# A gated cross-attention and FFN block on one core: the projection six slots behind instead of seven, and the last slots and the product stage's end in another order

## The chip, the core and the metric

The kernel runs on one of the eight cores of a Trainium2 chip. The core has five instruction queues: TensorE (PE in the profile; PEld is its weight load), VectorE (DVE), ScalarE (ACT), GpSimd (POOL) and SyncE (SP, which only issues transfers here). They run side by side and meet at semaphores. PSUM is the memory that TensorE writes into, SBUF the working memory. The metric is the device time of one execution in microseconds; the kernel before has a median of 463.42 us over 3 runs (462.39 to 464.57).

## What is computed

With x of 4 batches x 1024 rows x 256 columns and a context c of 4 x 154 x 256, cut from the reference:

```python
x = x + tanh(g_x) * xattn(layernorm(x), c, w_sim, b_sim, W_qv, b_qv)
x = x + tanh(g_f) * ffn(layernorm(x), w_gate, w_up, w_down)

# xattn(h, c): d = 256
Sim  = (h @ w1)[:, :, None] + (c @ w2)[:, None, :] + einsum('bid,bjd->bij', h * w3, c) + b_sim
A    = softmax(Sim, axis=2);  hq = A @ c
Batt = softmax(max(Sim, axis=2), axis=1);  hc = sum_i Batt_i h_i          # one row per batch
out  = concat([h, hq, h * hq, h * hc]) @ W_qv + b_qv

# ffn(y): weights quantized to 4 bits in blocks of 32, activations to 16 bits over the whole tensor
y = q16(y); up = q16(y @ q4(w_up).T); gate = q16(y @ q4(w_gate).T)
gate = q16(gate * u16(sigmoid(gate)));  o = q16(gate * up);  return o @ q4(w_down).T
```

Two things tie the stages together. The row `hc` of a batch needs the scores of all of the batch's 1024 rows before any of its rows can be projected. And each `q16` needs the largest magnitude of a whole 4096-row tensor before the next stage can begin.

## The kernel before, in words

**The attention stage** (to about 200 us) works in slots. A slot m has one pair of 128-row tiles at each step of a pipeline; there are N = 16 pairs, four to a batch, so slot m is place s = m mod 4 of batch b = m div 4. In a slot TensorE turns h of pair m (`turn_h`, line 521), scores pair m-1 (`score`, 535), turns the attention weights of pair m-2 (`turn_a`, 544), attends for pair m-3 (`attend`, 554), projects pair m-LAG (`project`, 566 to 570, twelve matrix products) and turns the normalized result of pair m-LAG-1 (`turn_y`, 609). LAG is 7. Each engine has a loop over the slots of its own, in which a fixed order of calls is written out; nothing is scheduled by a tool. Every engine takes its instructions strictly in that order, so a wait holds up all that stands behind it.

What VectorE does in a slot: `attended` (1135, the product h*hq of pair m-4), `residual` (1143 to 1154: x plus the projection, then mean and variance), `scored` (1119, bias and row maximum), `stats` (1081 to 1088), `normed` (1127), `norm_x1` (1160, the normalized yb) and `max_y` (1200). `row_std` and `y_std` (384, 388) are the reciprocal roots, which GpSimd takes; `bias_x` (439) adds the bias to x on GpSimd.

Once per batch: `batch_max` on VectorE (1206, 1208) makes a diagonal of the row maxima, `batch_max` on TensorE (629) spreads it, `batch_shift` (1212) reduces it, `batch_exp` on ScalarE (902) makes the weights, ScalarE and GpSimd multiply four rows of h each (908, 414), `row_pair` and `row_add` on GpSimd (421 to 431) sum them, `batch_cols` on TensorE (636, 637) sums over partitions, and `summary` on VectorE (1216 to 1224) makes the weights `we`, which the third part of each projection (570, or 601 in a batch's first pair) reads. A batch's first pair is projected in two parts, `project_first` (589, 591), which does not need `we`, and `project_rest` (601), which does.

In the gaps the FFN weights are quantized, one matrix m = 0, 1, 2 after the other: `weight_scales` (DVE 1238 to 1243), `weight_max` (PE 643), `weight_unit` (DVE 1248 to 1253), `weight_q` in two halves (POOL 401), `weight_values` (DVE 1258), `weight_f` (ACT 913) and `weight_n` (POOL 407). They stand in the slots that `W_AT` gives. One scale tile `wsc` serves all three. Then nine `turn_w` (PE 663) transpose the weights through three PSUM banks; ScalarE copies the high half out (918) and VectorE's `weight_part` (1264) makes the low half, which frees the bank for the `turn_w` three further on. `TURN_AT` says in which slots they stand.

**The hidden stages** (about 200 to 389 us) are three passes of 12 units of matrix products (731, 736): gate, up, and up once more, for the product. **The product stage** takes |up| of a unit (`up_int`, ACT 1020), its signs (DVE 1453) and the maximum of the product (DVE 1459, 1469). **The down stage** (from 396 us) quantizes chunks of 256 rows (ACT 1050/1054, DVE 1504 to 1509) and multiplies them with w_down (PE 766; the first chunk 777 and 782). Between the last hidden unit and the first chunk TensorE runs `WARM` = 22 products that nobody reads (803).

Of the kernel before, what the change touches and what calls it, by code (L numbers as in the profile page):

```python
# [38 lines left out]
P = 128  # L39
# [27 lines left out]
def build(nc, x, ctx, g_xattn, g_ffn, w_sim, b_sim, w_qv, b_qv, w_gate, w_up, w_down, out):  # L67
# [86 lines left out]
    wsc = place(a, "wsc", [P, NB], F32)  # L154
    wri = place(a, "wri", [P, NB], F32)
# [57 lines left out]
    with ExitStack() as stack:  # L213
# [29 lines left out]

        wchain, wall_rdy, wdiag_rdy, wm_ps, wri_rdy, wq_rdy, wqi_rdy, wqf_rdy, wn_rdy, wt_ps, wth_rdy, wt_rdy = map(
# [9 lines left out]
        gbank_ps, ubank_ps, aubank_rdy = map(sem, ("gbank_ps", "ubank_ps", "aubank_rdy"))  # L254
# [33 lines left out]
        TURNS = [(1, 0), (1, 1), (1, 2), (0, 0), (0, 1), (0, 2), (2, 0), (2, 1), (2, 2)]  # L288
        TURN_AT = {17: (0,), 19: (1, 2), 20: (3, 4, 5), 21: (6, 7, 8)}
# [87 lines left out]
        def _(pool):  # L377
# [17 lines left out]
            def weight_q(m, i):  # L395
# [5 lines left out]
                pool.tensor_tensor(wm, wm, wri[:, n].unsqueeze(2).broadcast_to([P, NB // 2, QB]), ALU.mult).then_inc(wq_rdy, 1)  # L401

            def weight_n(m):

                pool.wait_ge(wqf_rdy, m + 1)
                wm = wr[:, m, :].rearrange("p (n k) -> p n k", k=QB)
                pool.tensor_tensor(wm, wm, wsc[:].unsqueeze(2).broadcast_to([P, NB, QB]), ALU.mult).then_inc(wn_rdy, 1)  # L407
# [36 lines left out]
            for m in range(N + LAG):  # L444
                b, s = m // NP, m % NP
                if s == 3 and 4 <= m < N + 4:
                    for n in range(2):
                        bias_x(m - 5 + n)
                if s == 1 and 1 <= b <= B:
                    row_weigh(b - 1)  # L450
                if LAG <= m < L + LAG:
                    y_std(m - LAG)
                if s == 1 and 1 <= b <= B:
                    row_pair(b - 1)
                if s == 2 and 1 <= b <= B:
                    row_add(b - 1)
                if 1 <= m and m + 3 < N:
                    row_std(m + 3)
                if s == 0 and 4 <= m < N + 4:
                    for n in range(2):  # L460
                        bias_x(m - 4 + n)
                for i in range(3):
                    if m in (W_AT[i], W_AT[i] + 1):
                        weight_q(i, m - W_AT[i])
                    if m == W_AT[i] + 2:
# [30 lines left out]
        def _(pe):  # L496
            def turn_context(b):
                pe.wait_ge(cx_in[b], 16)
                ge(pe, ngm_rdy, b - 1)
                ge(pe, hc_rdy, b - 2)  # L500
# [130 lines left out]
            def batch_cols(b):  # L631

                pe.wait_ge(hs_rdy, b + 1)
                pe.wait_ge(cxT_rdy, min(b + 3, B))
# [10 lines left out]
            def turn_w(i):  # L645
# [3 lines left out]
                if i == 0:  # L649
                    pe.wait_ge(hT_rdy, N)  # L650
                elif i == 1:
# [26 lines left out]
            for m in range(N + LAG):  # L678
                b, s = m // NP, m % NP
                late = s == 3  # L680
                if LAG <= m and not late:
# [899 lines left out]
```

## Time and profile before

| | us |
|---|---|
| median of 3 runs | 463.42 |
| the profiled execution | 465.64 |
| its span, first to last instruction | 463.8 |
| TensorE busy | 436.0 (94%) |
| VectorE busy | 366.3 (79%) |
| ScalarE busy | 274.0 (59%) |
| GpSimd busy | 111.2 (24%) |
| mean granted TensorE clock | 0.982 |

Busy times are sums over instructions. TensorE's products overlap each other, and their ends are modelled, so its cost is best read from the starts of consecutive groups. The granted clock is the share of TensorE's full clock that it was given. The page's 40 slices show TensorE at 9 tenths or more nearly everywhere, with three places below: the first slice, the slices around 139 to 175 us (clock digits 8, 9, 6), and the slice at 390 us.

### The profile page before, as it was taken

Reading aid. Unit: us, or ns where it says so; the run is one execution under the profiler, and the core shown is the slowest. Engines: PE = TensorE matmul, PEld = TensorE weight load, DVE = VectorE, ACT = ScalarE, POOL = GpSimd, SP = SyncE. Lnnn points to the kernel's source line nnn. Section 1 sums busy time; section 2 is a strip of 40 time slices with the busy share of each in tenths; the row PEclk is TensorE's granted clock in tenths of the full one; section 3 lists DMA queues with packets and bytes.
Section 4 is the critical chain, followed back from the end, with each engine's and each line's share of the span. In section 5 each row is a group of like instructions: output and inputs, shape, how many; then the busy total and the mean of one; then the engine's idle time right before and its main releaser. Section 6 shows DMA issues by size and latency. Waiting matters only on the chain.

```text
span 463.8 us, 6761 instructions
## 1 busy us (share of the span) xinstructions
PE 436.0 (94%) x2430; PEld 299.2 (64%) x2430; DVE 366.3 (79%) x650; ACT 274.0 (59%) x342; POOL 111.2 (24%) x109
## 2 busy tenths in 40 slices
PE   4799999999997959999999999999999999899997
PEld 3788889799886848744444444444444444688886
DVE  5886789788785878886433789999898888798874
ACT  2677364457522312284334599998287777977760
POOL 1239275364743553100000013344000000000000
PEclk9999999999998969999999999999999999899999
DMA  7940002000200100110000000000000000344442
GB/s 243 315 155 1 0 2 91 1 0 6 87 1 0 65 28 0 38 54 0 0 0 0 1 1 1 0 0 0 1 0 0 0 0 1 114 137 137 136 136 69
DMA packets 20672, 21.13 MB, mean 46 GB/s; under 512 B 825, under 2 KB 20392, under 8 KB 20648
## 3 DMA queue, kind: packets, MB, share of 16 engines
q1 hardware_dynamic: 20628, 20.82, 14.2%
q8 instruction: 14, 0.23, 0.2%
q14 instruction: 10, 0.08, 0.1%
q10 hardware_dynamic: 20, 0.00, 0.0%
HBM read 12.43 MB, written 8.39 MB: 45 GB/s over the span
## 4 chain that ended last, share of the span: by engine, by line
PE 43%; DVE 26%; issue 20%; ACT 7%; POOL 4%; DMA 1%; ACTq 0%; POOLq 0%; DVEq 0%
PE ps L766 12%; PE ps L731 9%; PE ps L736 5%; DVE cols L1414 4%; DVE yb L1160 4%; PE ps L566 2%; PE ps L570 2%; PE ps L568 2%; PE ps L601 2%; DVE hid L1430 2%; ACT hid L991 2%; PE ps L554 1%; POOL wr L407 1%; POOL h L414 1%; ACT ag L996 1%
## 5 line engine op out<-in xcount | busy, mean ns | idle before, releaser
L731 PE MATMUL ps<-xh,wuh 128*128 128x512 f16 x192 | 72.8, 379 | 1.2 <-DVE gq L1453 1.1
L731 PE MATMUL ps<-xh,wul 128*128 128x512 f16 x192 | 72.8, 379 | 0.0
L736 PE MATMUL ps<-xl,wuh 128*128 128x512 f16 x192 | 57.1, 379 | 0.0
L1393 DVE TENSOR_REDUCE cols<-hid x10 | 22.9, 2286 | 24.3 <-ACT hid L968 24.3
L766 PE MATMUL ps<-wdl,oh 128*128 128x256 f16 x168 | 37.4, 273 | 0.0
L766 PE MATMUL ps<-wdh,oh 128*128 128x256 f16 x168 | 37.4, 273 | 0.0
L731 PE MATMUL ps<-xh,wgh 128*128 128x512 f16 x96 | 36.4, 379 | 0.0
L731 PE MATMUL ps<-xh,wgl 128*128 128x512 f16 x96 | 36.4, 379 | 0.0
L968 ACT ACTIVATE hid<-ps 128x2048 f32 x10 | 18.8, 1875 | 27.5 <-PE ps L736 27.5
L731 PEld LDWEIGHTS ps<-xh,wuh 128*128 (+1 forms) x192 | 18.8, 98 | 24.5 <-issue 2.2
L472 POOL PARTITION_ALL_REDUCE cols<-cols x4 | 1.5, 366 | 136.1 <-DVE cols L1353 130.0
L736 PEld LDWEIGHTS ps<-xl,wuh 128*128 (+1 forms) x192 | 18.8, 98 | 22.7
L731 PEld LDWEIGHTS ps<-xh,wul 128*128 (+1 forms) x192 | 18.8, 98 | 22.4
L1050 ACT ACTIVATE oq<-hid,cols 128x1536 int16 (+1 forms) x15 | 23.6, 1572 | 11.7 <-DVE ol L1509 11.7
L554 PE MATMUL ps<-aT,cx 77*128 77x256 f32 x128 | 30.5, 381 | 0.0
L1453 DVE TENSOR_TENSOR gq<-gq,ps 128x2048 bf16<-128x2048 int16 x11 | 25.2, 2287 | 6.0 <-ACT au L1020 6.0
L838 ACT ACTIVATE hT<-ps 128x512 f32<-128x512 f32 x16 | 9.5, 591 | 34.0 <-PE ps L521 34.0
L1430 DVE CUSTOM_DVE_ANT_0 hid<-ag,sq 128x2048 f32<-128x2048 int16 x12 | 29.2, 2435 | 0.2
L1414 DVE TENSOR_REDUCE cols<-ps 128x1 f32<-128x2048 f32 x12 | 27.4, 2286 | 1.6 <-PE ps L736 1.6
L736 PE MATMUL ps<-xl,wgh 128*128 128x512 f16 x96 | 28.6, 379 | 0.1
L1160 DVE TENSOR_SCALAR yb<-xa,cols 128x256 f32<-128x256 f32 x30 | 23.9, 836 | 5.4 <-POOL cols L388 5.4
L388 POOL TENSOR_TENSOR cols<-cols 128x2 f32<-128x2 f32 x15 | 11.7, 777 | 60.4 <-DVE cols L1154 60.4
(222 smaller groups left out, 1064.1 us busy)
## 6 DMA issues: line engine op xcount, KB each, us to landing
x_scratch<-xa SPq DMA_DIRECT2D x4, 1024.0 KB, 4.4
xo<-x_scratch SPq DMA_DIRECT2D x16, 256.0 KB, 2.7
out_dram<-xo SPq DMA_DIRECT2D x15, 256.0 KB, 2.2
xa<-in_x SPq DMA_DIRECT2D x3, 1024.0 KB, 12.6
xa<-in_x SPq DMA_DIRECT2D x4, 256.0 KB, 4.1
wv<-in_L_xattn_W_qv SPq DMA_DIRECT2D x1, 1024.0 KB, 8.5
wr<-in_L_ffn_w_gate SPq DMA_DIRECT2D x1, 768.0 KB, 10.2
wr<-in_L_ffn_w_up SPq DMA_DIRECT2D x1, 768.0 KB, 11.6
```

The lines of the kernel that those rows point to most:

```text
L388: pool.tensor_tensor(rstd2, vp2, mhalf[:, 0:2], ALU.pow).then_inc(rstd2_rdy, 1)
L554: mm = pe.matmul(hq_bank[:, d * PT:(d + 1) * PT], cx[b][0:JP, k, d * P:(d + 1) * P], aT[0:JP, n % 3, k, :], start=k == 0, stop=k == 1)
L731: pe.matmul(ps[hf][:, q, :], w_[:, d, ds(k * P, P)], xh[:, d, n], start=d == 0 and w_ is wh, stop=False)
L736: mm = pe.matmul(ps[hf][:, q, :], wh[:, d, ds(k * P, P)], xl[:, d, n], start=False, stop=d == KD - 1)
L766: mm = pe.matmul(down_ps(par)[:, t], o_[:, par, k, q], w_[:, k, :], start=not low and k == 0 and w_ is wdh, stop=low and k == KF - 1)
L968: act.activation(unit(hid, k, hf), ps_half(hf), ACT.Copy).then_inc(half_free[hf], 1)
L1050: act.activation(oq[:, par], hid[:, :, ds(c * CD, CD)], ACT.Copy, scale=c_co).then_inc(oqa_rdy, 1)
L1160: i_ = dve.tensor_scalar(yb[:, n % 2, t, :], xa[:, 2 * n + t, :], mv2[:, t, 0:1], rstd2[:, t:t + 1], ALU.subtract, ALU.mult)
L1393: dve.tensor_reduce(gmx[:, ds(k * 2 + hf, 1)], unit(hid, k, hf), AX.X, ALU.max, apply_absolute_value=True).then_inc(gm_done, 1)
L1414: dve.tensor_reduce(umx[:, u:u + 1], ps_half(u % 2), AX.X, ALU.max, apply_absolute_value=True).then_inc(half_free[u % 2], 1)
L1430: dve.tensor_tensor_reduce(half_of(hid, u), ag[:, u % 2, :], sq[u % 2][:], 1.0, 0.0, ALU.mult, ALU.max, pmx[:, u:u + 1]).then_inc(p_rdy, 1)
L1453: dve.tensor_tensor(g_.bitcast(BF16), g_, ps_half(hf), ALU.mult).then_inc(half_free[hf], 1)
```

## The change

The lag goes from 7 slots to 6, so the loops have 22 slots instead of 23. In slots 8, 12 and 16 (`ahead`) TensorE scores the batch's last pair before the projection and not behind it; VectorE, ScalarE and GpSimd take that pair's scores, `batch_max`, `batch_shift`, `batch_exp` and `row_weigh` first in the slot. `row_add` and `batch_cols` move from places 2 and 3 of the next batch to place 1, and a batch's first pair is projected in one piece at place 2, but for batch 0 (slot OPEN = 6), where `batch_cols` stands between its two parts. The scale tiles `wsc` and `wri` are doubled, and scales, values and norms of the three weight matrices have slots of their own. The nine `turn_w` now start with matrix 0 and stand in slots 18 to 20. At the product stage's end the eleventh |up| is taken bank by bank, the first down chunk is done in three groups of two blocks instead of two of three, and WARM is 24.

```diff
-        LAG = 7
+        LAG = 6
+        OPEN = NP + 2
         W_AT = [10, 14, 17]
+        SCALES_AT = [9, 13, 15]
+        VALUES_AT = [12, 16, 18]
+        NORMS_AT = [12, 17, 19]
-        WARM = 22
+        WARM = 24
-        TURN_AT = {17: (0,), 19: (1, 2), 20: (3, 4, 5), 21: (6, 7, 8)}
+        TURN_AT = {18: (0, 1), 19: (2, 3, 4), 20: (5, 6, 7, 8)}
...
+                ahead = s == 0 and 2 <= b <= B                 # TensorE's loop
+                if ahead:
+                    score(m - 1)
+                if LAG <= m and s == 2 and b <= B:
                     project_first(b - 1)
+                    if m != OPEN:
+                        project_rest(b - 1)
+                elif LAG <= m:
+                    project(m - LAG, b - 1 if ahead else None)
...
+                if s == 1 and 2 <= b <= B:
+                    batch_cols(b - 1)
...
+                if s == 0 and 1 <= b <= B:                     # GpSimd's loop
+                    row_weigh(b - 1)
                 if s == 1 and 1 <= b <= B:
-                    row_weigh(b - 1)
+                    row_add(b - 1)
...
+                if ahead:                                      # VectorE's loop
+                    scored(m - 1)
+                    batch_max(b - 1)
+                    if m + 3 < N:
+                        stats(m + 3)
+                    normed(m - 1)
+                    batch_shift(b - 1)
+                if LAG <= m and m != OPEN:
                     residual(m - LAG)
...
-            up_int(KF - 1, 0)                                  # ScalarE
+            for q in range(4):
+                act.wait_ge(ubank0_ps if q < 3 else unit_ps, q + 1 if q < 3 else 3 * NU - 1)
+                a_ = act.activation(au[:, 0, bank_of(q)], ps[0][:, q, :], ACT.Abs, scale=c_cu)
+            a_.then_inc(au_rdy, 1)
...
-            for g in range(2):
-                k = slice(g * KF // 2, (g + 1) * KF // 2)
+            for g in range(3):
+                k = slice(2 * g, 2 * g + 2)
```

TensorE, the end of slot 16 and the start of slot 17 before. L566 to L570 is the projection, L535 the scores, L544 `turn_a`, L554 `attend`, L609 `turn_y`, L629 `batch_max`:

```order
L570 MATMUL ps<-we,hT 128x256 x2
L535 MATMUL ps<-cp,hT 128x154 x4
L544 MATMUL ps<-ident,sc 77x128 x4
L554 MATMUL ps<-aT,cx_85 128x256 x4
L609 MATMUL ps<-ident,yb 128x128 x4
L566 MATMUL ps<-wv,hqT 128x256 x2
L568 MATMUL ps<-wv,prT 128x256 x2
L570 MATMUL ps<-we,hT 128x256 x2
L629 MATMUL ps<-diag,ones 128x128
```

and slot 16 in the changed kernel, whose lines have other numbers (L542 the scores, L573 to L577 the projection, L636 `batch_max`, L551 `turn_a`):

```order
L542 MATMUL ps<-cp,hT 128x154 x4
L573 MATMUL ps<-wv,hqT 128x256 x2
L575 MATMUL ps<-wv,prT 128x256 x2
L577 MATMUL ps<-we,hT 128x256 x2
L636 MATMUL ps<-diag,ones 128x128
L551 MATMUL ps<-ident,sc 77x128 x4
```

(the second half of the projection, the same three rows again, stands between the last two). Between the scores of a batch's last pair and `batch_max` there stood `turn_a`, `attend`, `turn_y` and half a projection; now there stands half a projection alone.

VectorE from slot 15 to `batch_max` of slot 16 in the changed kernel. L1220 is `max_y` of slot 15, L1263 to L1269 `weight_scales` of matrix 2, L1155 `attended`, L1139 `scored`, L1226 and L1228 `batch_max`:

```order
L1220 TENSOR_REDUCE cols<-yb 128x1
L1263 TENSOR_REDUCE wsc<-wr 128x48
L1265 TENSOR_SCALAR wsc<-wsc 128x48
L1266 TENSOR_REDUCE cols<-wsc 128x1
L1268 TENSOR_SCALAR wdiag<-ident,cols 128x128
L1269 RECIPROCAL wri<-wsc 128x48
L1155 TENSOR_TENSOR prT<-hqT,hT 128x2x256
L1139 ISA sc,cols<-ps,cbi 128x154
L1139 ISA cols 128x1
L1226 TENSOR_REDUCE cols<-cols 128x1
L1228 TENSOR_SCALAR diag<-ident,cols 128x128
```

and the same place before, from `scored` of slot 16 (L1119 is `scored`, L1206 and L1208 `batch_max`, L1258 `weight_values` of matrix 1, L1238 `weight_scales` of matrix 2):

```order
L1119 ISA sc,cols<-ps,cbi 128x154
L1119 ISA cols 128x1
L1206 TENSOR_REDUCE cols<-cols 128x1
L1208 TENSOR_SCALAR diag<-ident,cols 128x128
L1127 RECIPROCAL cols<-cols 128x2
L1160 TENSOR_SCALAR yb<-xa,cols 128x256 x2
L1200 TENSOR_REDUCE cols<-yb 128x1
L1258 TENSOR_SCALAR wqi<-wr 128x1536
L1238 TENSOR_REDUCE wsc<-wr 128x48
```

The scales of matrix 2 stood behind `batch_max` and now stand ahead of it.

VectorE in slots 19 and 20 of the changed kernel. L1290 is `weight_part` (wgl and wul are parts 2, 3, 4 in slot 19 and part 5 in slot 20, wdl parts 6 and 7), L1163 to L1174 `residual` of pair 14, L1180 and L1220 `norm_x1` and `max_y`:

```order
L1290 TENSOR_TENSOR wgl<-ps,wgh 128x2x256
L1290 TENSOR_TENSOR wul<-ps,wuh 128x2x256 x2
L1163 SCALAR_TENSOR_TENSOR xa<-ps,cols,xa 128x512
L1167 BN_STATS st<-xa 128x6 x2
L1171 BN_AGGR cols<-st 128x2 x2
L1174 TENSOR_SCALAR cols<-cols 128x2
L1180 TENSOR_SCALAR yb<-xa,cols 128x256 x2
L1220 TENSOR_REDUCE cols<-yb 128x1
L1290 TENSOR_TENSOR wul<-ps,wuh 128x2x256
L1290 TENSOR_TENSOR wdl<-ps,wdh 128x512 x2
```

The ninth `turn_w` waits for part 5. Before, part 5 stood in slot 20 and the ninth `turn_w` in slot 21; now both stand in slot 20.

## Rows read from the trace of the kernel before

**Rows 1.** Windows: start:end, length, PE, PEld, DVE, ACT, POOL busy (count), clock, DMA, GB/s.

```profile
27.70:128.30 100.60, 97.12 (x558) 86.45 (x557) 81.25 (x236) 57.59 (x151) 56.73 (x57) 1.00 0.07 24
...
396.30:401.90 5.60, 5.57 (x36) 4.36 (x37) 4.15 (x6) 5.60 (x5) 0.00 (x0) 0.70 0.25 81
```

**Rows 2.** Timeline of PE, slot 10: start, us, engine, line, operation, tiles, count.

```profile
67.05 1.03 PE L566 MATMUL ps<-wv,hqT 128*128 128x256 f32 x4
...
72.23 0.60 PE L521 MATMUL ps<-ident,h 128*128 128x128 f32 x4
72.67 1.22 PE L535 MATMUL ps<-cp,hT 128*128 128x154 f32 x8
73.72 0.60 PE L544 MATMUL ps<-ident,sc 128*77 128x128 f32 x4
74.16 1.89 PE L554 MATMUL ps<-aT,cx 77*128 77x256 f32 x8
75.89 0.60 PE L609 MATMUL ps<-ident,yb 128*128 128x128 f32 x4
```

**Rows 3.** Timeline of PE, from slot 16 to the attention stage's end.

```profile
128.27 1.03 PE L566 MATMUL ps<-wv,hqT 128*128 128x256 f32 x4
...
148.61 0.80 PE L643 MATMUL ps<-wdiag,ones 128*128 128x128 f32 x2 [3.33 <-DVE wdiag L1242]
...
164.69 0.61 PE L636 MATMUL ps<-ones,h 128*128 128x1 f32 x4 [2.81 <-POOL h L431]
...
169.48 3.78 PE L601 MATMUL ps<-we,hT 128*128 128x256 f32 x8 [3.05 <-DVE we L1224]
...
194.26 0.60 PE L609 MATMUL ps<-ident,yb 128*128 128x128 f32 x4
```

**Rows 4.** Timeline of DVE, slot 13, in which the scales of matrix 1 stand.

```profile
103.78 0.75 DVE L1143 SCALAR_TENSOR_TENSOR xa<-ps,cols,xa 128x512 f32<-128x512 f32 x1 [0.38 <-PE ps L570]
...
108.38 1.68 DVE L1160 TENSOR_SCALAR yb<-xa,cols 128x256 f32<-128x256 f32 x2 [0.64 <-POOL cols L388]
...
110.70 1.74 DVE L1238 TENSOR_REDUCE wsc<-wr 128x48 f32<-128x1536 f32 x1
...
113.50 0.63 DVE L1135 TENSOR_TENSOR prT<-hqT,hT 128x512 f32<-128x512 f32 x1
```

**Rows 5.** Timeline, GpSimd instructions beside VectorE's yb.

```profile
152.66 1.27 POOL L421 TENSOR_TENSOR h<-h 128x512 f32<-128x512 f32 x1
152.73 2.84 DVE L1160 TENSOR_SCALAR yb<-xa,cols 128x256 f32<-128x256 f32 x2 [1.14 <-POOL cols L388]
...
153.88 1.53 POOL L401 TENSOR_TENSOR wr<-wr,wri 128x768 f32<-128x768 f32 x1
...
176.07 2.78 POOL L407 TENSOR_TENSOR wr<-wr,wsc 128x1536 f32<-128x1536 f32 x1
176.44 2.88 DVE L1160 TENSOR_SCALAR yb<-xa,cols 128x256 f32<-128x256 f32 x2
```

**Rows 6.** Timeline of ACT and DVE: the cast, and residual to weight_part in slot 21.

```profile
170.33 1.48 ACT L913 ACTIVATE wr<-wqi 128x1536 f32<-128x1536 int16 x1 [3.27 <-DVE wqi L1258]
...
187.54 0.75 DVE L1143 SCALAR_TENSOR_TENSOR xa<-ps,cols,xa 128x512 f32<-128x512 f32 x1 [0.85 <-PE ps L570]
...
191.74 1.28 DVE L1264 TENSOR_TENSOR wdl<-ps,wdh 128x512 f16<-128x512 f32 x2
```

**Rows 7.** Timeline, the product stage's end and the first down chunk.

```profile
384.10 1.97 ACT L1020 ACTIVATE au<-ps,cols 128x2048 int16<-128x2048 f32 x1 [1.32 <-PE ps L736]
...
387.86 2.41 ACT L1036 ACTIVATE au<-ps,cols 128x512 int16<-128x512 f32 x4
...
388.98 4.91 PE L803 MATMUL ps<-wdl,wdh 128*128 128x512 f16 x22
396.33 0.28 PE L777 MATMUL ps<-wdh,oh 128*128 128x256 f16 x1 [2.44 <-DVE oh L1528]
...
401.94 0.27 PE L766 MATMUL ps<-wdh,oh 128*128 128x256 f16 x1
```

More of the change, by code:

```diff
@@ L688, in _ @@
                     turn_context(b + 1)
-                if 1 <= m <= N:
+                if 1 <= m < N and not ahead:
                     score(m - 1)
@@ L692, in _ @@
                     turn_a(m - 2)
-                if s == 1 and b == 1:
-                    batch_max(b - 1)
-                if s == 3 and 1 <= b <= B:
+                if m == OPEN:
                     batch_cols(b - 1)
@@ L740, in hidden_unit, with hidden @@
                 mm.then_inc(unit_ps, 1)
-            def hidden(wh, wl, done, first, bank_ps):
+            def hidden(wh, wl, done, first, bank_ps, bank0_ps=None):
                 with pe.Fori(0, KF - 1) as k:
@@ L924, in _ @@
                 b, s = m // NP, m % NP
+                ahead = s == 0 and 2 <= b <= B
+                if ahead:
+                    exps(m - 1)
+                    normed(m - 1)
+                    batch_exp(b - 1)
+                    row_weigh(b - 1)
                 if m < N:
@@ L934, in _ @@
                     turned_a(m - 2)
-                if 1 <= m <= N:
+                if 1 <= m < N and not ahead:
                     exps(m - 1)
@@ L940, in _ @@
                     attended(m - 3)
-                if 1 <= m <= N:
+                if 1 <= m < N and not ahead:
                     normed(m - 1)
-                if s == 1 and b == 1:
+                if m == NP:
                     batch_exp(b - 1)
-                if s == 1 and 1 <= b <= B:
                     row_weigh(b - 1)
@@ L1299, in _ @@
                 b, s = m // NP, m % NP
-                late = s == 3
+                ahead = s == 0 and 2 <= b <= B
                 if 4 <= m <= N + 3:
@@ L1325, in _ @@
                     stats(m + 3)
-                if 1 <= m <= N:
+                if 1 <= m < N and not ahead:
                     normed(m - 1)
-                if s == 1 and b == 1:
+                if m == NP:
                     batch_shift(b - 1)
-                if LAG <= m and not late:
+                if LAG <= m and m != OPEN:
                     norm_x1(m - LAG)
-                if s == 3 and 1 <= b <= B:
+                    max_y(m - LAG)
+                if m == OPEN or s == 1 and 2 <= b <= B:
                     summary(b - 1)
-                if LAG <= m and not late:
-                    max_y(m - LAG)
                 for i in range(3):
-                    if m == W_AT[i] - 1:
+                    if m == SCALES_AT[i]:
                         weight_scales(i)
```

127 lines of the change are left out of this document (65 added, 62 removed).

## The prediction, made before the changed kernel ran

> **What bounds the kernel now.** I read the page's slices first, then the windows, then TensorE's timeline. The slices show TensorE busy nearly throughout, so the question is where it is not, or where its clock is down. From 27.7 to 128.3 us it stands idle for 100.60 - 97.12 = 3.5 us at clock 1.00 [rows 1]. Behind that come three long waits: 3.33 us for the scales of matrix 2, 2.81 us for GpSimd's row sum and 3.05 us for the weights `we` [rows 3]. The clock goes down with them: the eight products of 169.48 last 3.78 us, and half of a slot's `attend`, which has as many of the same size, says 1.73 for eight at full clock [rows 2, 3].
>
> How much lies there, by counting. At full clock a projection costs 72.23 - 67.05 = 5.18 us, the scores 1.05, `attend` 1.73, and each group of four transposes 0.44 [rows 2]. From the start of slot 16 (128.27) before there remain seven projections (36.3), one score, two `turn_a` (0.9), three `attend` (5.2), seven `turn_y` (3.1), nine `turn_w` (3.9) and about 1.1 of small ones: 51.5 us. They end at 194.70, 66.4 us later [rows 3]. So 14.9 us are slack: 9.2 of waits named above, the rest mostly clock. By the same count the slots from 5 to 15 hold about 5 us. All of this is what a better order can win; behind it, until 389 us, TensorE has no gap that the change touches. The third place is the end of the product stage: TensorE waits 2.44 us for the first quantized block, then runs 36 products in 5.6 us at a granted clock of 0.70 [rows 1, 7].
>
> **The attention stage, part by part.** No arithmetic goes away: the same projections, scores and sums are issued, and the slot less at the end is one projection and one `turn_y` (5.62 us) more by slot 16. So the work counted from there falls from 51.5 to 45.9, and what matters is slack.
>
> Slots 5 to 15. Three waits go: the ones for `hc` and `we` in slots 11 and 15 (about 2.7 of the 5 us), since `batch_cols` now has 3.46 us of `project_first` behind it, more than the 2.4 of the summary. New are small ones. In slots 8 and 12 `batch_max` on TensorE comes 1.05 + 2.6 = 3.65 us after the slot's start, and VectorE, which ends the slot before late, has its diagonal ready after about 4.0 and 4.4: 0.4 + 0.75. In slot 13 `row_add` stands behind `weight_n` on GpSimd, which waits for values and cast of slot 12; I get the sum 1.7 us late. In slot 6 `batch_cols` is followed by one `attend` only, as cover for the summary, and GpSimd's `bias_x` is beside it: 1.5, and 0.8 around `batch_max` of slot 4, against 2.5 in these slots now. The sum is 5.2 against 5: no change, with bounds of -4 and +2 (all the new waits absent, or the two `bias_x` blocks in full).
>
> Slot 16. What bounds it is VectorE. Slot 15 holds the scales of matrix 2. In slot 13 now, scales that stand at this place are done 113.50 - 103.78 = 9.7 us after `residual` starts [rows 4]. There `norm_x1` was 0.6 late by GpSimd and slot 15 will be a little better, so about 9.2. The rest of slot 15 on TensorE is 4.1 us, so VectorE is free 5.3 us into slot 16, and `attended`, `scored` and `batch_max` take 0.65 + 0.6 + 0.45. The diagonal comes at 7.0, TensorE wants it at 3.65: 3.3 us of wait (2.3 to 4). The wait of 3.33 at 148.61 left about 1.3 of lowered clock behind it (0.2 to 1.7): I take 4.6 for both.
>
> Slot 18. `project_rest` waits for `we`. The path is y's root on GpSimd, `norm_x1`, `max_y`, `summary`. Behind the root GpSimd has `weight_n` (2.78) and at once `weight_q` (1.5). Where VectorE's yb pair, 0.73 alone, meets one such instruction it ends 0.5 behind that one's end (176.44 + 2.88 against 176.07 + 2.78); where it meets two in a row it ends with the second (155.57 against 155.41) [rows 5]. So here the pair takes 4.4 and not 0.75. From the end of slot 17's projection: `residual` 2.3 with its starts, with VectorE 0.8 late, root 0.7, pair 4.4, maximum 0.65, summary 1.2 = 10.1; TensorE reaches `project_rest` after 0.44 + 1.73 + 0.44 + 0.8 + 3.46 = 6.9. The wait is 3.2 (0 to 3.5: nothing if the pair isn't held), and 1.3 of clock: 4.5.
>
> The rule for this is in the Trainium skill, SBUF — State Buffer, section "SBUF: two separate sides": VectorE and GpSimd share a port pair as an exclusive lock, and whichever starts first holds it for the whole instruction. Had VectorE's yb the pair first, `weight_n` would be what waits and slot 18 would lose nothing; the trace is against that here, since the root and `weight_n` stand back to back on GpSimd while VectorE starts 0.37 later [rows 5]. The sum would be 4.5 lower by it.
>
> Slots 19 and 20. `weight_values` of matrix 2 stands in slot 18 behind a yb pair that two `bias_x` hold; the cast (1.48) [rows 6] stands before the first `turned_w` on ScalarE, so the first `weight_part` is some 10 us behind `project_rest`, and the fourth `turn_w` waits 0.7 for it. VectorE then starts slot 19's `residual` 2.9 late, `weight_n` of matrix 2 holds its yb pair for 2.9, and in slot 20 `turn_y` waits 1.05 and the next `turn_w` 1.0. Last, the ninth `turn_w` waits for part 5, which stands behind slot 20's `residual`. From a projection's end to the first part's end it is 192.4 - 187.33 = 5.05 us [rows 6]; TensorE gets there after 0.44 + 3 x 0.44 = 1.75. That is 3.3 if VectorE is on time, which nothing can hide; with VectorE's lateness I get 4.45. Clock 1.3. Together 8.5 (3.4 to 9.5).
>
> The attention stage: 128.27 + 5.62 + 0.2 + 45.9 + 4.6 + 4.5 + 8.5 = 197.6, against 194.7: 2.9 us later, or 2.7 without rounding. The chain behind it (last y, overall maximum, first hidden product) is the same.
>
> **The product stage's end.** The eleventh |up| takes 1.97 us after its unit's end [rows 7]; bank by bank only the last quarter, 0.6, and the unit's start, 0.1, is left. VectorE is then free only 0.7 before it starts now, so the gain is 0.7, and VectorE's two maxima carry it to the end. Three groups of two blocks instead of two of three make the first block ready 0.6 earlier. TensorE so starts at 395.05. The two more dummy products move their end from 393.9 to 394.3, so the gap falls from 2.44 to about 0.8. Gaps of 1.0 us in the attention stage left the clock at 1.00 [rows 1]. The first chunk's 36 products take 36 x 0.11 = 4.0 at full clock instead of 5.6, and TensorE starts the second chunk at 399.1 instead of 401.94 [rows 7]; from there it is the bound to the end. Gain 2.8, bounds 0.7 (clock falls as now, no gain from the groups) and 3.2.
>
> **Sum.** Attention +2.7, end -2.8: -0.1 us on the profiled execution's 465.64. That execution is 2.2 above the median; taking the difference over gives 463.4, and I say 463.5.
>
> **Rivals.**
>
> *VectorE keeps up (faster).* If GpSimd's instructions hold VectorE less than I have it, slot 16 costs 3.0 without a fall of the clock, slot 18 1.5, and slots 19 and 20 the 3.3 that can't be hidden with 1.3 of clock: 9.1 in place of 17.6. Then the time is 463.5 - 8.5 = 455, and with half of it 459. For it: VectorE is 79% busy only, and most of its late points rest on the yb pair. Against it: three pairs held for 1.7 to 2.9 us in the rows. I put it at 457.
>
> *The clock stays down (slower).* Four waits of 1 to 4 us fall within 50 us, where now three do. Behind the second pair of waits the clock cost 3.5 us and not 1.3. If each of three falls costs that, 6.6 come on top: 470; with VectorE a little earlier, 468. It decides from 2.3 us on, that is when more than one of the falls costs 3.5. Against it: the waits are some 12 us apart, not 5.
>
> *The clock falls in the first down chunk all the same.* Then the end gives 1.0 instead of 2.8: 465.3.
>
> **Chances.** Forecast 0.34, VectorE keeps up 0.30, the clock stays down 0.24, the down chunk gives nothing 0.12. What a measurement of this kernel can tell from no change is about 0.5%, 2.3 us. The first and the last case fall within it, bar 0.02 each way: faster 0.32, same 0.43, slower 0.25. The likeliest case alone spans 460.5 to 466.5. The range over the cases reaches from 456, into the faster rival, to 468.5, into the slower.
>
> **What would show it.** Right: in the changed kernel's timeline `batch_max` (L636) of slot 16 waits some 3 us for VectorE's diagonal with the scales (L1263) right ahead of it; `project_rest` of slot 18 (L608) waits for `we`; the ninth `turn_w` (L671) waits over 3 us for `weight_part`; the waits for `wdiag` and for the row sum are gone; the first down products run at clock 1.00. Wrong: if the ninth `turn_w` waits under 3 us, my reading of the order is wrong; if slot 18 has no wait, the lock is not what I make of it; if the attention stage ends before 192 us, VectorE had room that I didn't see.

## The result and the profile after

The changed kernel takes 468.87 us in the median (467.11 to 470.60, 4 runs), against 464.00 for the kernel before in the same comparison. The ratio is 1.0109 [1.0081, 1.0136]: some 5 us slower, just outside the range that was given, at the place of the slower rival. The two profiled executions stand closer than that: 467.11 after, the fastest of its four, and 465.64 before, slower than all four of the kernel before in this comparison (464.60 at most); that is +1.5 us. So two things want an explanation, the 1.5 us between the traces and the rest of the 5.

First the windows of the attention stage in the changed kernel, in the columns of [rows 1]: slots 5 to 15 up to 133.9, slots 16 to 21 up to the stage's end, and the first down chunk.

```profile
27.70:133.90 106.20, 102.37 (x584) 91.18 (x584) 84.22 (x256) 56.98 (x153) 55.42 (x58) 1.00 0.07 23
133.90:199.25 65.35, 52.36 (x258) 44.27 (x256) 46.84 (x89) 18.65 (x37) 25.28 (x23) 0.92 0.05 17
399.40:403.40 4.00, 3.91 (x36) 3.50 (x37) 3.76 (x9) 4.00 (x4) 0.00 (x0) 1.00 0.43 133
```

The first stretch is 5.6 us longer than in [rows 1], which is the one projection and `turn_y` that a lag of six slots puts there (5.62). The stage then ends at 199.25 where it ended at 194.70 [rows 3]: from slot 16 on there is one projection less to do and TensorE is busy for 52.4 us where it was busy for 57.2, yet the stretch is only 1 us shorter (65.35 us; before, from 128.30 to 194.70, 66.40).

Where the other 3.8 us went is in TensorE's timeline from slot 13 on.

```profile
114.46 0.61 PE L643 MATMUL ps<-ones,h 128*128 128x1 f32 x4 [1.62 <-POOL h L436]
...
140.70 0.49 PE L636 MATMUL ps<-diag,ones 128*128 128x128 f32 x2 [2.88 <-DVE diag L1228]
...
142.23 1.91 PE L575 MATMUL ps<-wv,prT 128*128 128x256 f32 x4
...
163.92 1.99 PE L608 MATMUL ps<-we,hT 128*128 128x256 f32 x8 [3.71 <-DVE we L1244]
...
175.86 1.22 PE L671 MATMUL ps<-ident,wr 128*128 128x128 f32 x8 [0.85 <-DVE wgl L1290]
...
190.29 1.09 PE L671 MATMUL ps<-ident,wr 128*128 128x128 f32 x4 [4.17 <-DVE wul L1290]
191.17 1.91 PE L573 MATMUL ps<-wv,hqT 128*128 128x256 f32 x4
...
196.22 1.03 PE L573 MATMUL ps<-wv,hqT 128*128 128x256 f32 x4
```

The waits of [rows 3] are gone, and three others of 2.9, 3.7 and 4.2 us have come, in slots 16, 18 and 20. Behind the first and the last of them four products take 1.91 us instead of 1.03: that is TensorE at the lower of its two clocks (1.2 in place of 2.4 GHz). Read by starts, the last projection takes 7.6 us and not 5.2. Behind the wait of 163.92 the eight products take 1.99, the full clock. A fall of the clock is thus no fixed part of a wait.

On VectorE and GpSimd stands what the waits are for. While TensorE waits in slot 16, VectorE has the scales of matrix 2 ahead of the diagonal, with the product h*hq and the scores between them. In slot 17 the two yb are held by two products of GpSimd back to back, and `we` stands behind them.

```profile
136.23 1.74 DVE L1263 TENSOR_REDUCE wsc<-wr 128x48 f32<-128x1536 f32 x1
...
140.35 0.29 DVE L1228 TENSOR_SCALAR diag<-ident,cols 128x128 f32<-128x128 f32 x1
...
157.56 4.34 DVE L1180 TENSOR_SCALAR yb<-xa,cols 128x256 f32<-128x256 f32 x2 [0.81 <-POOL cols L393]
...
162.98 0.88 DVE L1244 SCALAR_TENSOR_TENSOR we<-wv,cols 128x256 f32<-128x256 f32 x2
```

```profile
157.49 2.77 POOL L412 TENSOR_TENSOR wr<-wr,wsc 128x1536 f32<-128x1536 f32 x1
160.22 1.53 POOL L406 TENSOR_TENSOR wr<-wr,wri 128x768 f32<-128x768 f32 x1
```

The end of the product stage, to be held against [rows 7]:

```profile
393.32 5.34 PE L817 MATMUL ps<-wdl,wdh 128*128 128x512 f16 x24
399.49 0.28 PE L791 MATMUL ps<-wdh,oh 128*128 128x256 f16 x1 [0.83 <-DVE oh L1559]
...
403.43 0.27 PE L780 MATMUL ps<-wdh,oh 128*128 128x256 f16 x1
```

TensorE waits 0.83 us and not 2.44, and the first chunk takes 3.9 us at clock 1.00 instead of 5.6 at 0.70. From the start of the empty products to the span's end it is 465.3 - 393.32 = 72.0 us, before it was 463.8 - 388.98 = 74.8: 2.8 us won. So the two traces differ by +4.5 at the attention stage's end, by -0.2 in the hidden passes, and by -2.8 at the end.

### The profile page after: what moved, and what is told of

It is laid out like the page before. It is cut to its first block, busy times and chain, and to the rows that moved or that the text cites. A ratio compares the mean times of both kernels' runs of the same rounds, so it can differ in the third digit from the quotient of the medians.

```text
span 465.3 us, 6772 instructions
## 1 busy us (share of the span) xinstructions
PE 435.4 (94%) x2432; PEld 297.5 (64%) x2432; DVE 364.6 (78%) x652; ACT 275.0 (59%) x346; POOL 111.0 (24%) x109
## 4 chain that ended last, share of the span: by engine, by line
PE 47%; DVE 23%; issue 18%; ACT 8%; POOL 3%; DMA 1%; ACTq 0%; POOLq 0%; DVEq 0%
PE ps L780 12%; PE ps L745 9%; PE ps L750 4%; DVE cols L1444 4%; DVE yb L1180 4%; PE ps L575 3%; PE ps L573 3%; PE ps L577 3%; PE ps L561 2%; PE ps L542 2%; DVE hid L1460 2%; ACT hid L1008 2%; PE ps L608 2%; ACT ag L1013 1%; PE ps L596 1%
## 5 line engine op out<-in xcount | busy, mean ns | idle before, releaser
L1180 DVE TENSOR_SCALAR yb<-xa,cols 128x256 f32<-128x256 f32 x30 | 25.1, 878 | 8.6 <-POOL cols L393 8.6
L575 PE MATMUL ps<-wv,prT 128*128 128x256 f32 x96 | 26.4, 400 | 0.0
```

The source lines that it names most:

```text
L575: pe.matmul(o_, prT[:, par, d, q], wv[:, 2 * KD + d, :], start=False, stop=False)
L1180: i_ = dve.tensor_scalar(yb[:, n % 2, t, :], xa[:, 2 * n + t, :], mv2[:, t, 0:1], rstd2[:, t:t + 1], ALU.subtract, ALU.mult)
```

## The experiments

Each kernel ran with the kernel before on the same chip; the ratios are to that. Ratios are turned into us at 464.

| kernel | median us | ratio to before | mean clock over its runs |
|---|---|---|---|
| before (beside the first four) | 463.74 | 1 | 0.985 |
| changed kernel again | 469.36 | 1.0127 [1.0101, 1.0153] | 0.981 |
| end_only | 461.45 | 0.9953 [0.9933, 0.9974] | 0.988 |
| attn_only | 470.87 | 1.0161 [1.0133, 1.0189] | 0.981 |
| ninth_later | 463.99 | 1.0003 [0.9984, 1.0023] | 0.986 |
| max_behind | 465.78 | 1.0047 [1.0021, 1.0073] | 0.984 |
| summary_first | 467.08 | 1.0076 [1.0047, 1.0105] | 0.984 |
| norm_later | 469.16 | 1.0128 [1.0102, 1.0154] | 0.980 |
| filled | 465.46 | 1.0029 [1.0008, 1.0050] | 0.994 |
| filled_four | 464.19 | 0.9991 [0.9967, 1.0016] | 0.997 |
| before_filled | 462.50 | 0.9963 [0.9942, 0.9985] | 0.994 |
| end_warm22 | 461.94 | 0.9965 [0.9947, 0.9982] | 0.987 |
| three_fixes | 458.94 | 0.9885 [0.9847, 0.9924] | 0.990 |
| four_fixes | 455.41 | 0.9826 [0.9802, 0.9849] | 0.996 |
| five_fixes | 454.41 | 0.9799 [0.9774, 0.9824] | 0.994 |

### The same kernel again, and its two halves

The changed kernel without an edit:

> The changed kernel unchanged, to time it again beside the kernel before on the chip of the other three, and to have a second trace of it. Theory (waits and clock): the time is 466 to 470, and its trace shows the same five waits (slot 13 about 1.6 us, slot 16 about 2.9, slot 18 about 3.7, slot 20 about 4.2); where the time is above 467 the difference lies in stretches of lowered clock after these waits, before the first hidden pass. Rival (the clock is lowered at random or in the products' passes): a slower execution shows its lower clock outside the attention stage.

It took 469.36. TensorE's timeline of its profiled execution (469.27):

```profile
41.53 3.60 PE L608 MATMUL ps<-we,hT 128*128 128x256 f32 x8 [0.77 <-DVE we L1244]
...
115.84 0.61 PE L643 MATMUL ps<-ones,h 128*128 128x1 f32 x4 [1.64 <-POOL h L436]
116.56 2.06 PE L596 MATMUL ps<-wv,hqT 128*128 128x256 f32 x4
...
143.76 0.78 PE L636 MATMUL ps<-diag,ones 128*128 128x128 f32 x2 [2.89 <-DVE diag L1228]
144.33 1.91 PE L573 MATMUL ps<-wv,hqT 128*128 128x256 f32 x4
...
166.97 3.10 PE L608 MATMUL ps<-we,hT 128*128 128x256 f32 x8 [3.71 <-DVE we L1244]
...
194.45 0.63 PE L671 MATMUL ps<-ident,wr 128*128 128x128 f32 x4 [4.16 <-DVE wul L1290]
194.92 1.82 PE L573 MATMUL ps<-wv,hqT 128*128 128x256 f32 x4
```

These waits are those of the first trace to 0.02 us (only the 0.85 us of slot 19 is 0.28 here). What differs is the clock behind them: here it fell in slot 6 behind a wait of 0.77 us (eight products 3.60, in the first trace 1.99 behind the same 0.76), in slot 13, and in slots 16, 18 and 20. Five falls, where the first profile had two. Each costs 1.6 to 1.7 us when it is read by starts against the same groups at full clock, behind 0.77 us of wait as behind 4.16: 8.3 us in all. The two of the first trace cost 1.7 (slot 16) and 2.8 (slot 20). The stage ends at 202.22 and not at 199.25, the span at 467.4 and not at 465.3. The waits belong to the kernel, the falls to the execution. After the stage's end the clock is 1.00 in both, so the rival that put the lower clock there is out.

The end's part alone, put into the kernel before, and the changed kernel without it:

```diff
 end_only: before, with
-        WARM = 22
+        WARM = 24
-                for g in range(2):
+                for g in range(3):
-            up_int(KF - 1, 0)
+            for q in range(4):
+                act.wait_ge(ubank0_ps if q < 3 else unit_ps, q + 1 if q < 3 else 3 * NU - 1)
...
 attn_only: the changed kernel with these lines as before
```

> The kernel before with the product stage's end of the change alone (au of the last unit bank by bank, output scaling and down projection in thirds, 24 empty matmuls for 22). Theory: the last part shrinks by 2.8 us as in the two profiles, so 461.2 against 464.0, a ratio of 0.994, and the attention stage keeps its 194.7. Rival (the gain at the end belongs to the higher clock of that profile and is not the edit's): within 0.5 us of before. Second rival (a gain of the end is paid back by a clock that falls in the first down chunk): 463 to 464 with matmuls of doubled length behind the quantization.

> The changed kernel with the product stage's end of before: the attention stage's order alone. Theory: the whole loss of the change and the 2.8 us of the end on top, 469 to 472, first hidden pass at about 205 us; the last part as before, 74.8 us. Rival (the stages are not additive: the lost time in the medians comes from the end, where the profile happened to be a good one): 466 to 467.5.

461.45 and 470.87. The end wins 0.47% (2.2 us in the medians), the attention stage loses 1.61% (7.5 us), and -2.2 + 7.5 = 5.3 against the 5.9 of the whole in the same comparison: the halves add, within the intervals. The second rival for the end, a clock that falls in the first down chunk, is out: in end_only's profiled execution TensorE waits 0.82 us ahead of the chunk, whose 36 products then take 3.9 us at clock 1.00; in attn_only's it waits 2.43 us and the clock over the chunk is 0.72. Whether the two more empty products matter was asked of end_only with one number back:

```diff
-        WARM = 24
+        WARM = 22
```

> end_only with 22 empty matmuls ahead of the output's down projection as before, in place of 24. Theory (two matmuls of 0.2 us that fall into a wait and keep the clock up a little longer): within 0.5 us of end_only's 461.45. Rival (24 hold the clock through the first quarter of the down projection, 22 do not): 1 to 2.5 us slower than end_only, with doubled matmuls of the down projection's first chunk.

461.94, a ratio of 0.9965 against 0.9953, the intervals nearly cover each other. The gain is that of the banks and the groups; the empty products have no share that can be measured.

### Each wait by itself

The ninth transpose a slot later:

```diff
-        TURN_AT = {18: (0, 1), 19: (2, 3, 4), 20: (5, 6, 7, 8)}
+        TURN_AT = {18: (0, 1), 19: (2, 3, 4), 20: (5, 6, 7), 21: (8,)}
```

> The changed kernel with the ninth weight transpose put in slot 21 in place of slot 20, nothing else. Theory: the wait of 4.2 us for the weight part on VectorE in slot 20 goes or falls under 1 us, and the stretch of lowered clock behind it (matmuls of 1.8 to 1.9 us at the end of the stage, some 2.6 us lost) goes with it: first hidden pass 3.5 to 6.5 us sooner, time 462.5 to 465.5. Rival (VectorE is full there, the wait is only passed on to the next instruction that needs it): the wait moves to slot 21 or to the pass's start, and the time is within 1 us of the changed kernel's. Second rival (the ninth transpose and its split then stand ahead of the first hidden pass): 1.5 to 3 us of the gain are given back there.

```profile
188.96 1.82 PE L671 MATMUL ps<-ident,wr 128*128 128x128 f32 x12 [0.75 <-DVE wgl L1290]
190.62 1.03 PE L573 MATMUL ps<-wv,hqT 128*128 128x256 f32 x4
...
196.24 0.60 PE L671 MATMUL ps<-ident,wr 128*128 128x128 f32 x4
...
198.91 0.44 PE L624 MATMUL ps<-ident,yb 128*128 128x128 f32 x2 [0.56 <-DVE yb L1204]
```

463.99: one number in a table gives 1.24% back, 5.8 us, and the kernel is level with before. Slot 21 is also where the kernel before has its ninth transpose. The ninth transpose waits for nothing, the projection ahead of it runs at full clock, and of the two rivals only a wait of 0.56 us at the stage's end is left.

The maximum of slot 16 behind the projection:

```diff
-                    project(m - LAG, b - 1 if ahead else None)
+                    project(m - LAG, b - 1 if ahead and b < B else None)
+                    if ahead and b == B:
+                        batch_max(b - 1)
```

> The changed kernel with the matmul of slot 16 that turns the batch's maximum put behind the whole projection instead of inside it. Theory: the wait of 2.9 us for the diagonal goes, and with it the doubled matmuls behind it (1.8 us in the first profile); the maximum comes some 4 us later, which the row sums of the batch absorb or pass on to slots 17 and 18. If it is absorbed the time is 464.5 to 466 against 469.1; if it is passed on in whole, the column sums of slot 17 or `we` in slot 18 wait 2 to 4 us longer and the time is 468 to 470. I hold the first at 0.6.

```profile
142.62 0.49 PE L636 MATMUL ps<-diag,ones 128*128 128x128 f32 x2 [0.29 <-DVE diag L1230]
...
154.01 0.61 PE L643 MATMUL ps<-ones,h 128*128 128x1 f32 x4 [0.51 <-POOL h L436]
...
162.47 2.95 PE L608 MATMUL ps<-we,hT 128*128 128x256 f32 x8 [3.85 <-DVE we L1246]
```

465.78, 3.7 us won. The 2.9 us of wait shrink to 0.3; of the later maximum 0.5 comes back at the row sum and 0.14 at `we`.

The last batch's summary ahead of the norm of pair 11 (`norm_x1`), on VectorE in slot 17:

```diff
+                if m == NP * B + 1:
+                    summary(b - 1)
                 if LAG <= m and m != OPEN:
                     norm_x1(m - LAG)
                     max_y(m - LAG)
-                if m == OPEN or s == 1 and 2 <= b <= B:
+                if m == OPEN or s == 1 and 2 <= b < B:
                     summary(b - 1)
```

> The changed kernel with VectorE's summary of the last batch (sum, mean column, `we`) ahead of the norm of the eleventh tile and its scaled pair in slot 17. Theory: `we` is there some 4 us sooner, the wait of 3.7 us in slot 18 goes to under 0.8 us, while the scaled pair still takes 3 to 4 us beside GpSimd's two products but is needed only by the transpose behind the projection; time 464.5 to 466.5 against 469.1. Rival (VectorE is full from slot 16 on, an order inside it moves the wait only): the wait appears in front of the transposes of slot 18 or at the weight parts of slots 19 and 20, time within 1 us of 469.1.

First TensorE, then VectorE:

```profile
162.13 1.99 PE L608 MATMUL ps<-we,hT 128*128 128x256 f32 x8 [0.39 <-DVE we L1244]
...
176.28 1.84 PE L671 MATMUL ps<-ident,wr 128*128 128x128 f32 x8 [3.06 <-DVE wgl L1290]
```

```profile
158.64 3.44 DVE L1244 SCALAR_TENSOR_TENSOR we<-wv,cols 128x256 f32<-128x256 f32 x2
162.00 1.89 DVE L1180 TENSOR_SCALAR yb<-xa,cols 128x256 f32<-128x256 f32 x2
```

467.08, 2.4 us won, less than was expected of it (464.5 to 466.5). The wait of 3.7 us goes to 0.4 as it should, but the one in slot 19 grows from 0.85 to 3.1: TensorE reaches the transposes earlier, and the splits that they need are no earlier. Part of the rival was right. The rows show one thing more: it is now `we` that takes 3.44 us and not 0.88, since it is `we` that now meets GpSimd's product of 2.8 us.

That product, one slot later:

```diff
-        NORMS_AT = [12, 17, 19]
+        NORMS_AT = [12, 18, 19]
```

> The changed kernel with GpSimd's product of 2.77 us that norms weight matrix 1 in slot 18 instead of slot 17. Theory (VectorE's scaled pair is held by GpSimd's products beside it, and `we` queues behind the pair): in slot 17 only the half product of 1.5 us is left beside the pair, so the pair falls from 4.3 us to about 2 and the wait of slot 18 for `we` from 3.7 us to about 1.3; in slot 18 the product now stands beside the next pair, which grows from 2.6 us to about 5.4, and the weight parts behind it come 2.8 us later, so that slot 19 waits some 3.5 us where it waited 0.85. Net within 1.5 us of 469.1. Rival (the pair is long for a reason of its own): both pairs and the wait of slot 18 stay as they are.

TensorE, VectorE and GpSimd of it:

```profile
163.18 1.99 PE L608 MATMUL ps<-we,hT 128*128 128x256 f32 x8 [1.26 <-DVE we L1244]
...
176.98 1.80 PE L671 MATMUL ps<-ident,wr 128*128 128x128 f32 x8 [2.71 <-DVE wgl L1290]
```

```profile
159.28 1.88 DVE L1180 TENSOR_SCALAR yb<-xa,cols 128x256 f32<-128x256 f32 x2 [0.81 <-POOL cols L393]
...
170.69 0.69 DVE L1220 TENSOR_REDUCE cols<-yb 128x1 f32<-128x512 f32 x1
171.30 2.81 DVE L1284 TENSOR_SCALAR wqi<-wr 128x1536 int16<-128x1536 f32 x1
```

```profile
159.21 1.48 POOL L406 TENSOR_TENSOR wr<-wr,wri 128x768 f32<-128x768 f32 x1
...
170.47 2.82 POOL L412 TENSOR_TENSOR wr<-wr,wsc 128x1536 f32<-128x1536 f32 x1
```

The pair takes 1.88 us in place of 4.34 and the wait for `we` 1.26 in place of 3.71, as was worked out. In slot 18 I had the wrong victim: not the next pair (2.6 us, as it was) but the conversion behind it is held, 2.81 us. The maximum between the two, which stands beside the same product, is not held: it takes its usual 0.69. The splits are late by the conversion, slot 19 waits 2.7, and the time is the same, 469.16. This runs as the Trainium skill has it in SBUF — State Buffer, "SBUF: two separate sides", an exclusive lock between VectorE and GpSimd that lasts for the instruction: both 4.34 against 1.88 and 3.44 against 0.88 are the same instructions with and without the long product beside them. The 0.69 us of the maximum show that not every instruction of VectorE is held.

### The clock by itself

Empty products in the three long waits of the changed kernel, ahead of the waiting instruction; no wait is taken away:

```diff
+            def fill(bank, n):
+                for i in range(n):
+                    pe.matmul(bank[:, 0:P], ones[:], ident[:], start=True, stop=True)
...
+                        if largest_of == B - 1:
+                            pe.wait_ge(hT_rdy, N)
+                            fill(hT_bank, 13)
                         batch_max(largest_of)
...
+                    if b == B:
+                        fill(hT_bank, 16)
                     if m != OPEN:
                         project_rest(b - 1)
...
+                if i == 8:
+                    fill(m_bank, 18)
```

> The changed kernel with empty fp32 matmuls (128x128, results never read) put on TensorE ahead of its three long waits: 13 ahead of the batch maximum of slot 16, 16 ahead of the late half of the projection in slot 18, 18 ahead of the ninth weight transpose in slot 20. No wait is taken away. Theory (part of the loss is the clock that falls behind the waits): the three stretches of 3 to 4 us are filled, the matmuls behind them run at the full clock, and the time comes to 464 to 466.5 from 469.1, with the waited-for instructions starting within 0.3 us of where they start now. Rival (the lowered clock costs nothing, since VectorE sets the pace of the last slots): within 1 us of 469.1. Rival (the empty matmuls queue ahead of real ones and cost more than the clock gives): 470 or more.

```profile
116.60 1.91 PE L601 MATMUL ps<-wv,prT 128*128 128x256 f32 x4
...
135.67 1.22 PE L542 MATMUL ps<-cp,hT 128*128 128x154 f32 x8
...
160.02 3.73 PE L639 MATMUL ps<-ident,ones 128*128 128x128 f32 x32
163.90 1.99 PE L611 MATMUL ps<-we,hT 128*128 128x256 f32 x8
```

```profile
133.80:196.30 62.50, 60.07 (x361) 53.28 (x360) 47.62 (x94) 20.20 (x42) 26.99 (x24) 1.00 0.05 18
```

465.46, a ratio of 1.0029 against 1.0127: 4.5 us, without a single wait made shorter. From the end of `project_first` to the products with `we` it is 163.90 - 160.02 = 3.88 us, as it was with nothing in the wait. The window above holds the end of slot 15 too; slot 16 starts at 135.67 in this execution, since the clock fell in slot 13, whose wait is not filled, and cost 1.7 us. From slot 16's start to the stage's end at 196.30 it is 60.6 us at clock 1.00; in the first trace it was 65.2 (134.01 to 199.25) at 0.92. The difference of 4.6 us is what the two falls of the first trace cost (1.7 and 2.8).

What was still open is how much of this the kernel before loses too. So the same was done to its own three waits (14, 11 and 13 empty products ahead of lines 643, 636 and 601), and slot 13's wait was filled in the changed kernel:

```diff
 before_filled: before, with
+                if m == N + 3:
+                    pe.wait_ge(ngm_rdy, B)
+                    fill(m_bank, 11)
                 if s == 3 and 1 <= b <= B:
                     batch_cols(b - 1)
...
 filled_four: filled, with
+                if m == 13:
+                    pe.wait_ge(ngm_rdy, 3)
+                    fill(m_bank, 6)
                 if s == 1 and 2 <= b <= B:
                     batch_cols(b - 1)
```

> The kernel before with empty fp32 matmuls in its own three long waits: 14 ahead of the matrix' maximum in slot 17, 11 ahead of the column sums in slot 19, 13 ahead of the late half of the projection in slot 19. No wait is taken away. Theory (the change does not bring more clock loss of its own kind, it only moves waits; its waits are what is longer): the kernel before gains as much as the changed one did, some 4 us, to 459 to 460.5, and the difference of the two with filled waits is 5 us or more. Rival (the changed kernel loses more to the clock than the kernel before, since it has four falls where that has two or three): before gains 1 to 2.5 us only, to 461.5 to 463, and with filled waits the two differ by 2 to 3.5 us.

> filled with 6 more empty matmuls ahead of the column sums of slot 13, whose wait of 1.6 us was left open there. Theory (that wait too is followed by a lowered clock, some 2 us in most executions, as four_fixes gained by taking it away together with its wait): 1 to 2.5 us off filled's ratio of 1.0029, so 0.998 to 1.001 of before. Rival (four_fixes gained from the wait and its cover alone): within 0.5 us of filled.

filled_four took 464.19, another 0.38% (1.8 us, with intervals that overlap); its profiled execution has clock 1.0. In all the clock behind four waits costs the changed kernel 1.0127 - 0.9991, that is 6.3 us (5.5 by the first comparison's 1.0109). before_filled took 462.50, 1.7 us under before, as the rival had it. Its profiled execution, the slowest of its twelve (464.76), shows that its waits are not all covered, and that filling has a cost of its own:

```profile
159.91 2.62 PE L629 MATMUL ps<-ident,ones 128*128 128x128 f32 x22
164.42 0.97 PE L641 MATMUL ps<-ones,h 128*128 128x1 f32 x4 [1.88 <-POOL h L431]
...
166.56 5.34 PE L629 MATMUL ps<-ident,ones 128*128 128x128 f32 x26
171.74 1.89 PE L601 MATMUL ps<-we,hT 128*128 128x256 f32 x8
```

TensorE came 1.8 us sooner, GpSimd's row sum at the same time as in [rows 3] (164.42 and 164.69), so 1.9 us stayed idle and the clock fell once more, into the empty products. They then took 5.2 us by starts, and the products with `we` began at 171.74, though VectorE had `we` ready at 169.16 (166.71 + 2.45) and they had begun at 169.48 in [rows 3]: here the filling held up the work for some 2.5 us. For both reasons 1.7 us is a lower bound for what the clock costs the kernel before. With that said, the two filled kernels differ by 0.9991 - 0.9963, 1.3 us and not 5.9 (the rival had 2 to 3.5); their intervals leave this open between nothing and 3 us. The executions without any fall, at clock 1.000, say much the same, though the kernel before has only one: 460.53, against 462.28 in the mean of four of filled_four.

### Together

Three edits in one:

```diff
 TURN_AT of ninth_later, batch_max of max_behind, summary of summary_first
```

> The changed kernel with all three edits of order: the maximum of slot 16 behind the projection, the summary ahead of the norm in slot 17, the ninth transpose in slot 21. Theory (three waits of their own, each with its clock fall): the gains add to 8 to 11 us less what VectorE's load gives back, 458 to 461, below end_only's 461.45. Rival (the waits share one cause, a VectorE that is behind by its whole queue): each edit alone gains but together they stop at VectorE's own end, 462.5 to 464, as the ninth transpose alone gave.

458.94. Alone they gave 5.8, 3.7 and 2.4 us; together 1.0127 - 0.9885, 11.2 of the 11.8. So they don't share one late queue, as the rival had it. 

Then the product for matrix 0 behind the row sum of slot 13, and the splits of slot 18 ahead of the conversion of matrix 2:

```diff
 four_fixes: three_fixes, with
-        NORMS_AT = [12, 17, 19]
+        NORMS_AT = [13, 17, 19]
...
 five_fixes: four_fixes, with (ScalarE; VectorE's weight_part and weight_values likewise)
-                if m in VALUES_AT:
+                if m in VALUES_AT[:2]:
                     weight_f(VALUES_AT.index(m))
                 for i in TURN_AT.get(m, ()):
                     turned_w(i)
+                if m == VALUES_AT[2]:
+                    weight_f(2)
```

> three_fixes with the product that norms weight matrix 0 in slot 13 on GpSimd, behind the row sum, instead of in slot 12 ahead of it. Theory: the row sum of batch 2 ends 2.8 us sooner, the wait of 1.64 us in slot 13 goes, and the clock fall behind it with its 2 to 4 us of doubled matmuls: 454.5 to 457 against 458.94. Rival (something else holds the row sum, ScalarE's half of it): the wait stays over 1 us and the time within 0.5 us of three_fixes.

> four_fixes with the first two weight parts of slot 18 ahead of the third matrix' conversion, on ScalarE and on VectorE. In three_fixes ScalarE sat 6.5 us for the rounded values of matrix 2 with the two copies behind it, and slot 19 waited 3.1 us for the split. Theory: that wait goes with its clock fall of 1.8 us, 1 to 4 us off four_fixes. Rival (the conversion of matrix 2 is then late for the seventh transpose in slot 20): the wait reappears there, no gain.

GpSimd in slots 12 and 13 of three_fixes, and of four_fixes:

```profile
108.22 2.78 POOL L412 TENSOR_TENSOR wr<-wr,wsc 128x1536 f32<-128x1536 f32 x1 [2.95 <-ACT wr L929]
...
113.65 0.73 POOL L436 TENSOR_TENSOR h<-h 128x256 f32<-128x256 f32 x1
```

```profile
108.44 1.06 POOL L436 TENSOR_TENSOR h<-h 128x256 f32<-128x256 f32 x1
```

The row sum had stood idle behind the product of matrix 0, which waits 2.95 us for its cast. It is 4.9 us sooner now, the wait of slot 13 is gone (0.63 us for `we` is left in it), and the time is 455.41, 2.7 us by the ratios. The last edit takes the 3.1 us wait of slot 19 and leaves 1.5 us for a yb in its place: 454.41, 1.3 us by the ratios, the low end of what was expected, and the two intervals overlap. five_fixes is 2.0% faster than the kernel before, with the changed kernel's lag, its scores ahead and its end.

## Why the prediction was wrong, step by step

**Slots 5 to 15, no change.** Right in the first trace (106.20 - 100.60 = 5.6 against the 5.62 of work). The waits were sized a little high: 1.7 forecast and 1.62 found in slot 13, 0.75 and 0.41 in slot 12, 0.4 and 0.18 in slot 8, 1.5 and 1.27 in slot 6; in all 5.2 and 3.8, and the 5 us that I had counted for the kernel before were 3.5 as well. Wrong was what I put at nothing: a fall of the clock behind the 0.77 us of slot 6 and the 1.6 us of slot 13, as in the second trace, 1.6 to 1.7 us each. I had argued, for the product stage's end, that gaps of 1.0 us left the clock at 1.00 in [rows 1]; they may, and in another execution they don't.

**Slot 16, 4.6 us.** 2.88 us of wait, and 1.7 us, read by starts, of products at the lower clock: 4.6.

**Slot 18, 4.5 us.** 3.71 us of wait and no fall in the first trace; forecast 3.2 and 1.3. The pair was to take 4.4 us and took 4.34, and norm_later shows that it was held for the reason given.

**Slots 19 and 20, 8.5 us.** 0.85, 0.63, 0.76 and 4.17 us of waits and 2.5 of clock: 8.9. The ninth transpose waits 4.17, forecast 4.45.

**The attention stage, +2.7 us.** In the trace +4.55. The three places hold 17.2 us, where I had 17.6. What is left of the stretch from slot 16 on is 65.35 - 17.2 = 48.2, where I had counted 45.9: some 2.3 us more. Each of the six waits costs some 0.15 us more between starts than its row says, some groups of weight transposes take over 0.5 us and not 0.44, and the ninth took 0.88 at the lower clock.

**The product stage's end, -2.8 us.** -2.8 in the traces, -2.2 [-3.1, -1.2] in the medians by end_only. The rival that the first down chunk falls all the same is out.

**The sum, -0.1 on the profiled time.** This is the step that failed, and in it the term for the clock: +1.5 between the profiled executions, and +5 to +6 between the medians. Two terms were mis-sized, the 2.3 us of counted work above and, the greater one, the clock. I had put 1.3 us of lowered clock behind each of three waits, 3.9 in all, taken from one row of one execution, and nothing behind the waits of slots 6 and 13. The second trace, whose clock of 0.982 is that of most executions, has five falls of 1.6 to 1.7 us, 8.3 in all; by the medians the clock behind four of the waits costs 6.3 us (filled_four against the changed kernel). The kernel before loses 4.7 us by the same reading of its trace (1.6 behind the wait at 148.61, 3.1 behind the one at 169.48), and filling its waits gave 1.7. So the change made the loss to the clock greater by 3.6 (the two traces) to 4.6 us (the fillings, where 1.7 is a lower bound and 4.6 an upper one), and that is most of the 5 to 6. Of the 4.7 us of the kernel before, before_filled shows that the first 1.6 end in the wait for the row sum; the rest it could not win in the execution shown, since the clock fell again in the filling. The profile of the changed kernel happened to be one with two falls and that of the kernel before one of its slower ones, so the +1.5 between them is luck and no support for the forecast.

**The rival "the clock stays down", 468.** It gave the time, 468.87, and the right thing, the clock. Its mechanism was a little off: I let each of three falls cost 3.5 us. Single falls cost 1.6 to 2.8 us here, and there are up to five of them; too few falls and too dear ones came to nearly the same sum, so that the time fits this well is in part luck. "VectorE keeps up" is out, since every wait came in full.

What is not settled: why the same wait is followed by a fall in one execution and not in the next, and how the 1.3 us that the filled kernels differ by divides between waits and work.

## What to carry to other kernels

A wait of TensorE costs its length and then, in a share of the executions, a stretch of lowered clock, here mostly 1.6 to 1.7 us whether the wait had been 0.77 or 4.16 us long; when waits are moved about, count how many there are and not only their sum, and compare clocks over several executions before a profile's difference is taken for the kernel's. Look for the one late instruction that stands in a queue ahead of something that TensorE needs sooner: each of the five edits of order here moves one or two calls or one number, and together they take 3.3% off the changed kernel, 15 us. And where a long product of GpSimd runs, put beside it on VectorE what nobody waits for, or what it does not hold: the pair, `we` and the conversion were held here, the maximum was not. Filling a wait with empty products is no free gain either: where the clock falls into them they end after what was waited for.

## What the hardware showed that I had not expected

The same wait, 0.76 and 0.77 us in slot 6, was followed in one execution by eight products in 1.99 us and in another by the same in 3.60. Empty 128x128 fp32 products in waits of 2.9 to 4.2 us, with nothing else changed, raised the granted clock from a mean of 0.981 to 0.994 and took 4.5 us off 469. The same filling bought the kernel before only 1.7 us for about as much clock (0.983 to 0.994): in the execution shown, 1.6 us of TensorE's time were won ahead of a wait that did not move, and the empty products behind it ran some 2.5 us over.
